# Moving the first chunk's key reads to ScalarE, and a stack clear and a split to GpSimd, in the prologue of an attention-and-experts kernel

## The chip, the cores and the metric

The kernel runs on one core of one Trainium2 chip. The metric is the device time of one launch in microseconds (us), as the median of several runs. Before the change three runs gave 858.39, 859.47 and 859.04 us, a median of 859.04 us.

## The reference, cut to what matters

One block of a gated cross-attention layer and a routed expert layer, on 32 sequences of 128 tokens and width 128, all in float32:

```python
x = x + tanh(g_xattn) * xattn(layernorm(x), ctx, ...)
x = x + tanh(g_ffn) * ffn(layernorm(x), ...)

def xattn(x, xa, ...):                  # 16 heads of 8
    q, k, v    = heads(x @ Wqkv + bqkv)
    _, ka, va  = heads(xa @ Wqkv_aux + bqkv_aux)
    p, pa = softmax(q k' / sqrt(8)), softmax(q ka' / sqrt(8))
    out = (p v) * (1 - sigmoid(g)) + (pa va) * sigmoid(g)
    return out @ Wo + bo
def ffn(x, ...):                        # 64 experts of width 64, top 8 of 4 groups, and a shared one
    return sum_e w[:, e] * (silu(x @ Wg[e]) * (x @ Wu[e])) @ Wd[e] + shared(x)
```

Only the attention, and of it only its first sequences, is touched by the change.

## The kernel before

The 32 sequences are taken in 16 pairs; `n` is a pair, `b = 2n + c` a sequence. The attention runs over all pairs first, the experts follow. Each of the five engine queues (`on_sp`, `on_pool`, `on_act`, `on_dve`, `on_pe`) is a list written out by hand. Each engine takes its list strictly in order and waits on semaphores, so an instruction that waits holds back everything behind it on its engine, DMA issues included.

**What a pair needs.** The layer norm of x (`norm_stats`, `root` with its power on GpSimd, `norm`), a transpose on TensorE (`transposes`) evacuated by ScalarE (`evac_t`), and the projections `project_qk`, `project_ka`, `project_v`. ScalarE copies q and k out of PSUM (`copy_q`, `copy_k`) and, for the first two pairs, also ka (`copy_first_ka`). The scores are computed from bf16 parts: `split` takes a float32 tile apart into three bf16 parts with four instructions in a row (L1167, L1170, L1172, L1174 on VectorE; L609, L612, L614, L616 on GpSimd). A pair has three splits: one of q, and one of k and ka for each of its two sequences. Each counts `lo_ok` up by one.

**The stacks.** The parts go to a DRAM scratch and come back in the order in which the score matmuls want them, in `stack_q[s]` and `stack_k[s]`, three buffers of each. Pair 0 is the "first chunk": its parts are stored by `store_first_q`, `store_first_k(c)` and read back by `load_first(c)`, four `load_products` calls of two DMAs each (L414 and L417) for one sequence: q of head half 1, q of half 0, k of half 1, k of half 0. Pair 1 follows in the same queue with `store_q(1, 1)`, `store_k(1, 1)`, `load_stack_q(1)`, `load_stack_k(1)`. All of these are issued by SyncE, one behind the other. Before their first load the stacks are filled once with zeros or with `kones`: `stack_k[0]` and `stack_k[1]` by VectorE (`clear_stack`, L936), the q stacks and the third k stack by ScalarE.

**The prologue** is what lies ahead of the first `body`. TensorE computes the scores of sequences 0 and 1 (`first_scores`, L1308, four rounds each), VectorE takes the maxima of each round (`first_maxima`, L997) and from them the shift of the exponent (`minus_max`, L1005), and one round's scores must wait until the maxima of the round before the last are taken. The first `body` begins on TensorE with the shifted scores of sequence 0 (`shifted`, L1323), laced with the scores of sequence 2 (`scores`, L1294). For these it waits on three things:

```python
            if c == 0:
                wait(pe, stk[S_HEAD[u] // HH][s], 64 * ...)      # stack_there(2, 0): half 1 of pair 1's stacks
            if j == 0:
                wait(pe, mx_ok, UNITS * b + u - 1)               # scores(2, 0, 0): all maxima of sequences 0 and 1
            if u == 0 and j == 0:
                wait(pe, shift, 16 * (b + 1))                    # shifted(0, 0, 0): the shift rows of sequence 0
```

`clear_v(1)` on GpSimd sets the second buffer `V` to zero (L640) and its columns of ones; `gate_consts` on VectorE makes the gates that GpSimd then multiplies into `wo` (L656, L660). These are needed by `bias_of_v`, in the second quarter of the first body.

Of the kernel before, what the change touches and what calls it, by code (L numbers as in the profile page):

```python
# [16 lines left out]
F32 = mybir.dt.float32  # L17
# [7 lines left out]
P = 128  # L25
# [146 lines left out]
def attention(nc, sem, m, m_cw, psum, v):  # L172
# [131 lines left out]
    q_first, k_first = sem("first_q_parts_stored"), [sem(f"first_k_parts_stored{c}") for c in range(CH)]  # L304
# [66 lines left out]

    def weight_loads(sp):

        sp.dma_start(wqkv[:], v["Wqkv"].rearrange("d (o n) -> d o n", o=3)).then_inc(w_qkv_in, 16)
        sp.dma_start(wqkva[:], v["Wqkv_aux"].rearrange("d (o n) -> d o n", o=3)).then_inc(w_qkv_in, 16)

    def bias_loads(sp):

        turned = lambda a: a.rearrange("(h d a) -> d h a", d=DH, a=1)
        for i, b in enumerate((turned(v["bqkv"][0:P]), turned(v["bqkv"][P:2 * P]), turned(v["bqkv_aux"][P:2 * P]))):  # L380
            sp.dma_start(bcol[:, i:i + 1], b, allow_slow_non_contiguous=True).then_inc(c_in, 16)

# [9 lines left out]
    def on_sp(sp):  # L392
# [17 lines left out]
        def load_products(to, rows, keys, half, width, done):  # L410
            own = rows[:, half * width:(half + 1) * width]
            mixed = own if keys else own[DH:]
            step = DH if keys else 0
            sp.dma_start(to[0:4 * DH], bass.AP(mixed.tensor, mixed.offset,  # L414
                                               [[2 * width, 2 * DH], [step * 2 * width, 2], [1, width]])).then_inc(done, 16)
            plain = own[DH:3 * DH] if keys else own[0:2 * DH]
            sp.dma_start(to[4 * DH:6 * DH], plain).then_inc(done, 16)  # L417

        def load_stack_q(n):

            s = n % NST
            wait(sp, st_mm, UNITS * CH * (n - NST + 1))
            wait(sp, q_st[n % 2], 16 * ((n + 1) // 2))
            for half in (1, 0):
                load_products(stack_q[s][PARTS_AT[half]:PARTS_AT[half] + ROWS_S].rearrange("p h c t -> p (h c t)"),
                              q_v[n], False, half, HH * TC, stk[half][s])

        def load_stack_k(n):

            s = n % NST  # L430
            wait(sp, st_mm, UNITS * CH * (n - NST + 1))
            wait(sp, k_st[n % 2], 16 * ((n + 1) // 2))
            for half in (1, 0):
                load_products(stack_k[s][PARTS_AT[half]:PARTS_AT[half] + ROWS_S].rearrange("p h c a t -> p (h c a t)"),
                              k_v[n], True, half, 2 * HH * TC, stk[half][s])

        def store_first_q():

            wait(sp, lo_ok, 1)
            for c in range(CH):  # L440
                src = parts_q[0][:, :, c * P:(c + 1) * P]
                sp.dma_start(q0_d[c].rearrange("s p t -> p s t"), src).then_inc(q_first, 16)
# [6 lines left out]

        def load_first(c):  # L450

            wait(sp, q_first, 32)
            for half in (1, 0):
                load_products(q_of(0)[PARTS_AT[half]:PARTS_AT[half] + ROWS_S, :, c].rearrange("p h t -> p (h t)"),
                              q0_v[c], False, half, HH * P, stk0[half][c])
            wait(sp, k_first[c], 16)
            for half in (1, 0):
                load_products(k_of(0)[PARTS_AT[half]:PARTS_AT[half] + ROWS_S, :, c].rearrange("p h a t -> p (h a t)"),
                              k0_v[c], True, half, 2 * HH * P, stk0[half][c])
# [106 lines left out]
    def on_pool(pool):  # L566
# [28 lines left out]
        def split(n, half, c):  # L595
# [7 lines left out]
            if n == 2 and half == 0:  # L603
                wait(pool, q_first, 32)
# [43 lines left out]
        root(1)  # L648
        pool.wait_ge(xn_ok, 2)
        root(2)  # L650
        pool.wait_ge(lo_ok, SPLITS * 2)
# [11 lines left out]
        clear_v(1)  # L663
        pool.memset(f_mhalf[:], -0.5).then_inc(fc_ok, 1)
        pool.wait_ge(fc_ok, 1)
        pool.memset(f_gtop[:], HIGH).then_inc(fc_ok, 1)
# [51 lines left out]
    def on_act(act):  # L718
# [130 lines left out]
        copy_k(1)  # L849
        copy_first_ka(1)  # L850
        act.wait_ge(v_zero, 3)
# [67 lines left out]
    def on_dve(dve):  # L919
# [12 lines left out]
        def clear_stack(i):  # L932

            for a in range(2):
                one_col = kones[:, 2 * a:2 * a + 2].bitcast(F32).unsqueeze(1).to_broadcast([P, HH * CH, P // 2])
                ins = nc.vector.tensor_copy(stack_k[i][:].rearrange("p h c a t -> p (h c) a t")[:, :, a, :].bitcast(F32), one_col)  # L936
            ins.then_inc(stack_zero, 1)
# [253 lines left out]
        split(1, 1, 1, 1)  # L1191
        for r in range(ROUNDS):
            first_maxima(0, r)
        minus_max(0, 0, 3)
# [53 lines left out]
    def on_pe(pe):  # L1248
# [162 lines left out]
        wait(pe, t_ev, 2)  # L1411
        transposes(2, 0)
        first_scores(0, 0)
# [696 lines left out]
```

## Time and profile before

| what | value |
|---|---|
| median of 3 runs | 859.04 us |
| the profiled execution's own time | 859.58 us |
| its span in the profile | 857.8 us |
| TensorE busy | 826.2 us, 96% of the span |
| VectorE / ScalarE / GpSimd busy | 683.6 / 566.8 / 637.3 us |
| share of TensorE in the chain that ended last | 87% |
| start of the first `body` on TensorE | 36.43 us |

The span is what the hardware profiler saw between the first and the last instruction; the execution's own time has 1.8 us more around it. A row of the timeline gives start, duration (both us), engine, line, operation, what it writes and reads, a count when like instructions were merged, and in brackets how long the engine stood idle before it and what released it. "SPq" and "ACTq" are DMA issues of SyncE and ScalarE.

### The profile page before, as it was taken

The page shows a single profiled execution, that of the slowest core. Times are in us where ns is not written, and L with a number is a line of the kernel's source. Part 1 is how long each engine was busy: PE and PEld are TensorE (multiplying, and loading weights), DVE is VectorE, ACT ScalarE, POOL GpSimd, SP SyncE. Part 2 cuts the span into 40 slices and gives each one's busy share as a digit, 9 for nine tenths or more (in the row PEclk, how much of TensorE's full clock was granted, in tenths as well). Part 3 has the DMA queues.
Part 4 walks back from the last instruction along what each step waited for, and adds up shares of the span by engine and source line. Part 5 has one row for each costly group of instructions (what it writes and reads, how often), then busy time and mean ns, then how long its engine had stood idle before and what let it go on. Part 6 is the DMA issues. An engine that isn't in the chain of part 4 may idle for free.

```text
span 857.8 us, 20206 instructions
## 1 busy us (share of the span) xinstructions
PE 826.2 (96%) x6733; PEld 646.0 (75%) x6733; DVE 683.6 (80%) x1648; ACT 566.8 (66%) x964; POOL 637.3 (74%) x602
## 2 busy tenths in 40 slices
PE   4899999999999999999999999999999999999997
PEld 3477777777766678888888888878888888888885
DVE  6789999999897769769678877867966977876665
ACT  4388888888878665575576576557557557655554
POOL 2668888888854378877787786777777788778785
PEclk8599999999999999999999999999999999999999
DMA  4677786776652167447456554654654755546562
GB/s 119 173 169 173 178 183 155 187 169 170 160 126 51 53 152 169 120 111 184 117 142 147 131 142 125 154 135 109 163 139 111 171 130 134 149 116 150 137 138 58
DMA packets 108036, 120.04 MB, mean 140 GB/s; under 512 B 28560, under 2 KB 70352, under 8 KB 106496
## 3 DMA queue, kind: packets, MB, share of 16 engines
q1 hardware_dynamic: 105056, 118.23, 57.5%
q10 hardware_dynamic: 2880, 0.59, 0.4%
q8 instruction: 49, 0.80, 0.4%
q14 instruction: 51, 0.42, 0.2%
HBM read 103.55 MB, written 14.71 MB: 138 GB/s over the span
## 4 chain that ended last, share of the span: by engine, by line
PE 87%; DVE 5%; DMA 3%; issue 2%; SPq 1%; ACT 1%; POOL 0%; DVEq 0%; POOLq 0%
PE bank L1999 20%; PE bank L2000 20%; PE bank L2001 20%; PE bank L1336 7%; PE bank L1323 5%; PE bank L1294 3%; PE bank L1276 2%; PE bank L1344 2%; PE bank L1260 1%; PE bank L1357 1%; DVE mx L989 1%; PE bank L1270 1%; DMA cwb<-wts_scratch 1%; DMA stack_q<-nmaxT 1%; PE bank L1976 1%
## 5 line engine op out<-in xcount | busy, mean ns | idle before, releaser
L1676 POOL TENSOR_TENSOR hid<-act,cwb 128x512 f32<-128x512 f32 x264 | 424.0, 1615 | 126.4 <-DVE act L1903 69.1
L1729 ACT ACTIVATE silu<-bank 128x512 f32<-128x512 f32 x256 | 152.9, 597 | 190.7 <-PE bank L2001 189.9
L1903 DVE TENSOR_TENSOR act<-silu,bank 128x512 f32<-128x512 f32 (+1 forms) x264 | 180.5, 684 | 119.5 <-ACT silu L1729 78.7
L1999 PE MATMUL bank<-xhi,weights_hi 128*128 128x512 f32 x520 | 206.6, 397 | 0.0
L1911 DVE TENSOR_TENSOR hlo<-hid,hhi 128x512 fp32r<-128x512 f32 x256 | 197.5, 772 | 8.5 <-ACT hhi L1735 8.3
L2001 PE MATMUL bank<-xlo,weights_hi 128*128 128x512 f32 x520 | 204.2, 393 | 0.0
L2000 PE MATMUL bank<-xhi,weights_lo 128*128 128x512 f32 x520 | 203.9, 392 | 0.0
L1735 ACT ACTIVATE hhi<-hid 128x512 fp32r<-128x512 f32 (+1 forms) x264 | 164.8, 625 | 15.7 <-POOL hid L1676 13.1
L989 DVE TENSOR_REDUCE mx<-bank 128x4 f32<-128x512 f32 x240 | 156.0, 683 | 16.6 <-PE bank L1294 14.8
L786 ACT ACTIVATE prob<-bank 128x1024 f32<-128x1024 f32 x128 | 131.2, 1025 | 48.6 <-PE bank L1323 46.5
L2001 PEld LDWEIGHTS bank<-xlo,weights_hi 128*128 128x128 f32 x520 | 97.6, 188 | 22.0
L1999 PEld LDWEIGHTS bank<-xhi,weights_hi 128*128 128x128 f32 x520 | 97.6, 188 | 21.3 <-ACT silu L1729 0.4
L2000 PEld LDWEIGHTS bank<-xhi,weights_lo 128*128 128x128 f32 x520 | 97.8, 188 | 20.3
L1999 PE MATMUL bank<-hhi,weights_hi 128*128 128x512 f32 x256 | 101.1, 395 | 4.5 <-DVE hlo L1911 4.4
L2000 PE MATMUL bank<-hhi,weights_lo 128*128 128x512 f32 x256 | 100.3, 392 | 0.0
L2001 PE MATMUL bank<-hlo,weights_hi 128*128 128x512 f32 x256 | 99.9, 390 | 0.0
L1323 PE MATMUL bank<-stack_q,stack_k 52*128 52x128 bf16 (+1 forms) x1024 | 80.0, 218 | 7.4 <-DMA stack_k<-k_scratch 2.7
L1323 PEld LDWEIGHTS bank<-stack_q,stack_k 52*128 52x128 bf16 (+1 forms) x1024 | 58.0, 94 | 33.6 <-issue 13.9
L1336 PE MATMUL bank<-prob,V 128*32 128x128 f32 x2048 | 82.5, 279 | 0.1
L1294 PE MATMUL bank<-stack_k,stack_q 52*128 52x256 bf16 (+1 forms) x480 | 74.8, 274 | 0.4 <-DVE mx L989 0.2
L1336 PEld LDWEIGHTS bank<-prob,V 128*32 128x32 f32 x2048 | 48.1, 109 | 17.9 <-issue 11.1
L1999 PEld LDWEIGHTS bank<-hhi,weights_hi 128*128 128x128 f32 x256 | 48.0, 187 | 17.8 <-DVE hlo L1911 6.6
(238 smaller groups left out, 1022.1 us busy)
## 6 DMA issues: line engine op xcount, KB each, us to landing
cwb<-wts_scratch SPq DMA_DIRECT2D x174, 384.0 KB, 5.4
stack_k<-k_scratch SPq DMA_DIRECT2D x30, 256.0 KB, 4.3
k_scratch<-parts_k SPq DMA_DIRECT2D x15, 384.0 KB, 3.4
stack_q<-q_scratch SPq DMA_DIRECT2D x30, 128.0 KB, 2.9
stack_k<-k_scratch SPq DMA_DIRECT2D x30, 128.0 KB, 5.2
q_scratch<-parts_q SPq DMA_DIRECT2D x15, 192.0 KB, 2.7
xin<-in_x_dram SPq DMA_DIRECT2D x16, 128.0 KB, 3.0
cin<-in_ctx_dram SPq DMA_DIRECT2D x16, 128.0 KB, 3.1
```

The costliest lines, as they stand in the source:

```text
L786: act.activation(prob[pair % RP][:].rearrange("p u k -> p (u k)"), wide[:], ACT.Exp, scale=scale).then_inc(p_ok, 1)
L989: nc.vector.tensor_reduce(mx[par][:, 2 * f:2 * f + 2, h:h + 2].rearrange("p a h -> p h a"), s_bank[u % 2][:].rearrange("p (h a k) -> p h a ...
L1323: ins = nc.tensor.matmul(st_bank[u % 2][:, j * P:(j + 1) * P], k_of(n)[at, h % HH, c, a, :], q_of(n)[at, h % HH, c, :], start=True, stop=True)
L1336: ins = nc.tensor.matmul(o_bank[par][VW * j:VW * (j + 1), (u // 2) * P:(u // 2 + 1) * P], V[i][:, a, par, h0 + j, :], prob[(ROUNDS * b + u ...
L1676: pool.tensor_tensor(h_buf[k][:], a_buf[k][:], cwb[slot][:, q % GP, :], ALU.mult).then_inc(h_ok, 1)
L1729: act.activation(s_buf[k % RS][:], g_bank[k % 2][:], ACT.Silu).then_inc(s_ok, 1)
L1735: act.activation(hhi[k % RH][at], h_buf[k % RS][at], ACT.Copy).then_inc(hh_ok, 1)
L1903: nc.vector.tensor_tensor(a_buf[k % RS][at], s_buf[k % RS][at], u_bank[k % 3][at], ALU.mult).then_inc(a_ok, 1)
L1911: nc.vector.tensor_tensor(hlo[k % RH][:], h_buf[k % RS][:], hhi[k % RH][:].bitcast(F32), ALU.subtract).then_inc(hl_ok, 1)
L1999: nc.tensor.matmul(bank, w[0], mh, start=first, stop=False)
L2000: nc.tensor.matmul(bank, w[1], mh, start=False, stop=False)
L2001: return nc.tensor.matmul(bank, w[0], ml, start=False, stop=last)
```

## The change

- `load_products` becomes a helper with the issuing engine as argument; `load_first(c)` is replaced by `load_first_q(eng, c, half)` and `load_first_k(eng, c, half)`. `store_first_q` counts one semaphore for each sequence, so that a q read waits for its own sequence's store only.
- ScalarE issues three of the four key reads of the first chunk: (0, half 1) between `copy_k(1)` and `copy_first_ka(1)`; (0, half 0) and (1, half 1) after it. SyncE keeps the four q reads and the key read (1, half 0), and `store_first_k(1)` moves up to stand behind the first q read.
- GpSimd clears `stack_k[1]` with two copies and then does `clear_v(1)` and the `f_` memsets, all right after `root(1)`; VectorE no longer does `clear_stack(1)`.
- GpSimd takes the last split of pair 1 (`split(1, 1, 1)`); VectorE keeps the other five of pairs 0 and 1. `split(1, 1, 0, 0)` moves ahead of `norm_stats(2)`, `split(1, 1, 1, 0)` ahead of `norm(2)`, and `gate_consts` behind the first round of maxima.
- TensorE does `first_scores(0, 0)` ahead of `transposes(2, 0)`.

```diff
+    def load_products(eng, to, rows, keys, half, width, done):
+        own = rows[:, half * width:(half + 1) * width]
+        mixed = own if keys else own[DH:]
+        step = DH if keys else 0
+        eng.dma_start(to[0:4 * DH], bass.AP(mixed.tensor, mixed.offset,
+                                           [[2 * width, 2 * DH], [step * 2 * width, 2], [1, width]])).then_inc(done, 16)
+        plain = own[DH:3 * DH] if keys else own[0:2 * DH]
+        eng.dma_start(to[4 * DH:6 * DH], plain).then_inc(done, 16)
+
+    def load_first_q(eng, c, half):
+        wait(eng, q_first[c], 16)
+        eng.wait_ge(stack_clear, 1)
+        load_products(eng, q_of(0)[PARTS_AT[half]:PARTS_AT[half] + ROWS_S, :, c].rearrange("p h t -> p (h t)"),
+                      q0_v[c], False, half, HH * P, stk0[half][c])
+
+    def load_first_k(eng, c, half):
+        wait(eng, k_first[c], 16)
+        eng.wait_ge(stack_zero, 1)
+        load_products(eng, k_of(0)[PARTS_AT[half]:PARTS_AT[half] + ROWS_S, :, c].rearrange("p h a t -> p (h a t)"),
+                      k0_v[c], True, half, 2 * HH * P, stk0[half][c])
+    def one_rows(i, a):
+        to = stack_k[i][:].rearrange("p h c a t -> p (h c) a t")[:, :, a, :].bitcast(F32)
+        return to, kones[:, 2 * a:2 * a + 2].bitcast(F32).unsqueeze(1).to_broadcast([P, HH * CH, P // 2])
...
@@ on_sp
         store_first_q()
         store_first_k(0)
+        load_first_q(sp, 0, 1)
+        store_first_k(1)
+        load_first_q(sp, 0, 0)
+        load_first_q(sp, 1, 1)
+        load_first_q(sp, 1, 0)
+        load_first_k(sp, 1, 0)
         sp.wait_ge(stack_zero, 2)
         sp.wait_ge(stack_clear, 2)
-        load_first(0)
-        store_first_k(1)
-        load_first(1)
         store_q(1, 1)
         store_k(1, 1)
@@ on_pool
         root(1)
+        pool.wait_ge(kones_rows, 1)
+        pool.wait_ge(stack_zero, 1)
+        for a in range(2):
+            ins = pool.tensor_copy(*one_rows(1, a))
+        ins.then_inc(stack_zero, 1)
+        clear_v(1)
+        pool.memset(f_mhalf[:], -0.5).then_inc(fc_ok, 1)
+        pool.wait_ge(fc_ok, 1)
+        pool.memset(f_gtop[:], HIGH).then_inc(fc_ok, 1)
         pool.wait_ge(xn_ok, 2)
         root(2)
-        pool.wait_ge(lo_ok, SPLITS * 2)
+        pool.wait_ge(lo_ok, SPLITS * 2 - 1)
+        split(1, 1, 1)
...
@@ on_act
         copy_k(1)
+        load_first_k(act, 0, 1)
         copy_first_ka(1)
+        load_first_k(act, 0, 0)
+        load_first_k(act, 1, 1)
         act.wait_ge(v_zero, 3)
         copy_v(0, 0)
         evac_t(2, 0)
@@ on_dve
-        clear_stack(0)
+        clear_stack()
         norm_stats(1)
         norm(1)
-        clear_stack(1)
         split(0, 0, 0, 0)
         split(0, 0, 1, 0)
         split(0, 0, 1, 1)
+        split(1, 1, 0, 0)
         norm_stats(2)
-        split(1, 1, 0, 0)
+        split(1, 1, 1, 0)
         norm(2)
-        gate_consts()
-        split(1, 1, 1, 0)
-        split(1, 1, 1, 1)
         for r in range(ROUNDS):
             first_maxima(0, r)
+            if r == 0:
+                gate_consts()
@@ on_pe
+        first_scores(0, 0)
         transposes(2, 0)
-        first_scores(0, 0)
         first_scores(0, 1)
```

## Rows read from the trace of the kernel before

**Rows 1.** The profile's page: chain that ended last, shares by engine.

```profile
PE 87%; DVE 5%; DMA 3%; issue 2%; SPq 1%; ACT 1%; POOL 0%; DVEq 0%; POOLq 0%
```

**Rows 2.** Chain that ended last, in order of time: start, us, what.

```profile
21.71 0.56 SPq L414
...
31.96 4.42 DMA stack_k<-k_scratch
36.43 0.28 PE bank L1323
```

**Rows 3.** Timeline, maxima of sequences 0 and 1 on VectorE.

```profile
26.38 2.36 DVE L997 TENSOR_REDUCE mx<-bank 128x8 f32<-128x1024 f32 x2 [0.61 <-PE bank L1308]
...
32.94 2.36 DVE L997 TENSOR_REDUCE mx<-bank 128x8 f32<-128x1024 f32 x2
```

**Rows 4.** Timeline, TensorE between the projections and the third round of scores.

```profile
18.80 1.22 PE L1276 MATMUL bank<-wqkv,xcT 128*128 128x128 f32 x4 [0.56 <-ACT full_k L766]
...
20.67 0.63 PE L1253 MATMUL bank<-ident,xn 128*128 128x128 f32 x2
...
22.27 1.89 PE L1308 MATMUL bank<-stack_k,stack_q 52*128 52x256 bf16 x8 [0.54 <-DMA stack_k<-first_k_scratch]
...
24.09 1.22 PE L1260 MATMUL bank<-xcT,wqk 128*128 128x256 f32 x2
...
25.24 1.88 PE L1308 MATMUL bank<-stack_k,stack_q 48*128 48x256 bf16 x8
```

**Rows 5.** Timeline, ScalarE's copies out of PSUM.

```profile
12.89 0.47 ACT L766 ACTIVATE full_k<-bank,bcol 128x256 f32<-128x256 f32 x1 [0.36 <-PE bank L1270]
...
16.43 0.47 ACT L761 ACTIVATE full_k<-bank,bcol 128x256 f32<-128x256 f32 x1 [1.36 <-DVE parts_k L1174]
...
18.28 0.47 ACT L766 ACTIVATE full_k<-bank,bcol 128x256 f32<-128x256 f32 x1 [1.38 <-PE bank L1270]
```

**Rows 6.** DMA issues one by one: KB, us from issue to landing.

```profile
first_k_scratch<-parts_k SPq DMA_DIRECT2D x1, 192.0 KB, 2.0
...
stack_k<-first_k_scratch SPq DMA_DIRECT2D x1, 64.0 KB, 3.2
```

**Rows 7.** Timeline, DMA issues of SyncE and ScalarE.

```profile
14.97 0.36 SPq L448 DMA_DIRECT2D first_k_scratch<-parts_k  x1
...
30.05 1.44 ACTq L780 DMA_DIRECT2D stack_q<-nmaxT  x1
37.97 0.63 ACTq L780 DMA_DIRECT2D stack_q<-nmaxT  x1
```

**Rows 8.** Timeline, VectorE's first splits, those of pair 0.

```profile
11.85 0.29 DVE L1167 CAST parts_q<-full_q 128x256 bf16<-128x256 f32 x1
...
15.97 0.43 DVE L1174 TENSOR_TENSOR parts_k<-rest,parts_k 128x256 bf16<-128x256 f32 x1
```

**Rows 9.** Timeline, GpSimd: what its kinds of work cost.

```profile
1.55 0.29 POOL L572 CAST ident_bf<-ident 128x128 bf16<-128x128 f32 x1
...
9.39 0.70 POOL L582 TENSOR_TENSOR rstd<-var,mhalf 128x2 f32<-128x2 f32 x1 [3.26 <-DVE var L974]
...
17.42 0.70 POOL L582 TENSOR_TENSOR rstd<-var,mhalf 128x2 f32<-128x2 f32 x1 [7.33 <-DVE var L974]
...
24.33 1.80 POOL L640 MEMSET V<- 128x2048 f32 x1
...
33.20 0.61 POOL L609 TENSOR_TENSOR parts_k<-full_k,ones 128x256 bf16<-128x256 f32 x1
```

**Rows 10.** Timeline, a small VectorE instruction without and beside GpSimd work.

```profile
290.08 0.17 DVE L1797 TENSOR_SCALAR f_negm<-f_mv 128x4 f32<-128x4 f32 x1
...
361.60 1.80 POOL L1676 TENSOR_TENSOR hid<-act,cwb 128x512 f32<-128x512 f32 x1 [0.24 <-DVE act L1903]
362.57 0.86 DVE L1797 TENSOR_SCALAR f_negm<-f_mv 128x4 f32<-128x4 f32 x1
```

**Rows 11.** Windows of 1 us: length, busy time of PE, PEld, DVE, ACT, POOL, granted clock, DMA.

```profile
39.00:40.00 1.00, 1.00 (x14) 0.78 (x13) 0.00 (x0) 0.00 (x0) 0.00 (x0) 0.59 0.07 16
```

More of the change, by code:

```diff
@@ L303, in attention @@
     k_st = [sem(f"k_parts_stored{i}") for i in range(2)]
-    q_first, k_first = sem("first_q_parts_stored"), [sem(f"first_k_parts_stored{c}") for c in range(CH)]
+    q_first, k_first = ([sem(f"first_{n}_parts_stored{c}") for c in range(CH)] for n in "qk")
     stk0 = [[sem(f"first_stack_half{a}_loaded{c}") for c in range(CH)] for a in range(2)]
@@ L408, in store_k @@
             sp.dma_start(k_d[n].rearrange("s p c a t -> p s (c a t)"), parts_k[i][:]).then_inc(k_st[i], 16)
[L410 to L417, printed above, removed]
         def load_stack_q(n):
@@ L424, in load_stack_q @@
             for half in (1, 0):
-                load_products(stack_q[s][PARTS_AT[half]:PARTS_AT[half] + ROWS_S].rearrange("p h c t -> p (h c t)"),
+                load_products(sp, stack_q[s][PARTS_AT[half]:PARTS_AT[half] + ROWS_S].rearrange("p h c t -> p (h c t)"),
                               q_v[n], False, half, HH * TC, stk[half][s])
@@ L433, in load_stack_k @@
             for half in (1, 0):
-                load_products(stack_k[s][PARTS_AT[half]:PARTS_AT[half] + ROWS_S].rearrange("p h c a t -> p (h c a t)"),
+                load_products(sp, stack_k[s][PARTS_AT[half]:PARTS_AT[half] + ROWS_S].rearrange("p h c a t -> p (h c a t)"),
                               k_v[n], True, half, 2 * HH * TC, stk[half][s])
@@ L441, in store_first_q @@
                 src = parts_q[0][:, :, c * P:(c + 1) * P]
-                sp.dma_start(q0_d[c].rearrange("s p t -> p s t"), src).then_inc(q_first, 16)
+                sp.dma_start(q0_d[c].rearrange("s p t -> p s t"), src).then_inc(q_first[c], 16)
         def store_first_k(c):
@@ L448, in store_first_k @@
             sp.dma_start(k0_d[c].rearrange("s p a t -> p s (a t)"), src).then_inc(k_first[c], 16)
[L450 to L459, printed above, removed]
         def expert_weights(g, j):
@@ L603, in split @@
             if n == 2 and half == 0:
-                wait(pool, q_first, 32)
+                for done in q_first:
+                    wait(pool, done, 16)
             elif n == 2:
@@ L662, in on_pool @@
         pool.wait_ge(wo_ok, 4)
[L663 to L666, printed above, removed]
         pool.wait_ge(fc_ok, 2)
@@ L930, in shift_rows_of_k, with clear_stack @@
             dve.wait_ge(kones_rows, 1)
-        def clear_stack(i):
+        def clear_stack():
             for a in range(2):
-                one_col = kones[:, 2 * a:2 * a + 2].bitcast(F32).unsqueeze(1).to_broadcast([P, HH * CH, P // 2])
-                ins = nc.vector.tensor_copy(stack_k[i][:].rearrange("p h c a t -> p (h c) a t")[:, :, a, :].bitcast(F32), one_col)
+                ins = nc.vector.tensor_copy(*one_rows(0, a))
             ins.then_inc(stack_zero, 1)
```

## The prediction, made before the changed kernel was run

> **What bounds the kernel now.** I read the page first. The chain that ended last is TensorE for 87% of the span [rows 1], so after the prologue the kernel is a belt of matmuls: what starts it earlier ends it earlier, one for one. Everything that the change touches lies ahead of the first body or at its edge, so I then read the chain in order of time up to there. It runs through SyncE's issues of the first chunk's reads, which begin with the DMA issue at 21.71 us, through the store and reload of pair 1, and ends in a read of `stack_k` that is issued at 31.96 and lands 4.42 us later; TensorE begins the body at 36.43 [rows 2]. The second question is what would come next if that read came early. The body also waits for the last maxima of sequences 0 and 1. They are done at 32.94 + 2.36 = 35.30, and from the third round of sequence 0 at 26.38 on VectorE works without a gap worth naming, 8.92 us for this stretch [rows 3]. So the queue of SyncE gives at most 36.43 - 35.35 = 1.08 us, and more only if the maxima come earlier too.
>
> The maxima hang on TensorE [rows 4]: the values of pair 0 are projected from 18.80, as soon as ScalarE's second ka copy is out [rows 5], the third transposes follow at 20.67, the first scores at 22.27 after 0.54 us idle for a read of `stack_k`, a projection at 24.09, and the third round of scores at 25.24. Two rounds of scores take 24.09 - 22.27 = 1.82, one 0.91; four transposes about 0.86 (two of them start 0.43 after the other two); the projection 1.15.
>
> **The change part by part.** I count time from how late VectorE has finished the three splits of pair 0. Before, that is at 15.97 + 0.43 = 16.40 [rows 8]. Call the lateness against 16.40 after the change D. ScalarE's `copy_k(1)` waits for it (16.43), the ka projection waits for that, and the second ka copy at 18.28 for the projection [rows 5], so D moves this whole chain.
>
> (a) Key reads on ScalarE, with D = 0. The store of the parts of sequence 0 is issued at 14.97 [rows 7] and lands 2.0 us later [rows 6], at 16.97. ScalarE's copy ends at 16.90, so it waits 0.07 us. An issue on ScalarE takes 0.63 [rows 7], so two end at 18.2, just ahead of 18.28, when the ka copy can go: nothing is lost behind them. The second is issued at 17.6 and lands 3.2 us later [rows 6], at 20.8. The four issues after the ka copy end at about 21.3; behind them stand `copy_v(0, 0)`, whose matmuls end near 20.9, and `evac_t(2, 0)`, which is not due before 22.7. They are covered. If an issue takes 1.44 us, as one of ScalarE's does [rows 7], the read lands at 21.6 and the ka copy is 0.8 late: a cost of 0.8 us at most; I take nothing, since only one of the two rows is that long.
>
> (b) First scores ahead of the third transposes. TensorE is through with the values at 20.67 [rows 4]; the scores start at 20.8. Then 0.91 + 0.86 + 0.91, and the projection starts at 23.48 instead of 24.09: 0.61 us earlier. The transposes need the norm of pair 2: VectorE is at that point with one more split and the two norms, by 20.85, against a need at 21.7; covered by 0.85 us. The third round of scores and the last maxima move with the projection, to 35.30 - 0.61 = 34.69. `gate_consts` (0.55 us) lies between the first and the second round of maxima, while TensorE transposes; without that cover it would cost its 0.55.
>
> (c) SyncE's queue. It is free of the first chunk's reads near 21.9 instead of 26.6, the store of pair 1's keys waits for GpSimd's split (four instructions of about 0.65 with gaps, 2.8 us, instead of 1.5 on VectorE, ended near 23.2), and even with the longest reload shown, 4.42 us [rows 2], the half that the body wants lands near 31.4. It is off the path by 3 us, and every us of D moves both. So the maxima decide, and the body starts at 34.75: a gain of 1.68 - D. The later GpSimd work (`wo`, the splits of pair 2) is either earlier or hangs on the same projection.
>
> (d) The clear and the memsets on GpSimd, which is where D comes from. VectorE loses the clear that stood ahead of its q split, which may start with ScalarE's q copy near 11.4 instead of at 11.85 [rows 8]; but the k split behind it waits for the ka copy that ends at 12.89 + 0.47 = 13.36 [rows 5], as it did before, so the saving ends there: D is never below 0. GpSimd is through with `root(1)` at 10.09 [rows 9] and then copies twice 128x1024. The trace has no such copy. From below: a memset of 2048 elements takes 1.80 us [rows 9], 0.9 for 1024. From above: a two-input instruction of 256 takes 0.61 [rows 9], 2.4 us for 1024. A one-input cast of 128 takes 0.29 [rows 9], near the memset's rate and a small fixed part, so I take 1.05 us each: 10.15 to 12.25. Then comes the memset of `V`, 1.80.
>
> Does that hold VectorE up? A tensor_scalar of 4 elements takes 0.17 us with GpSimd idle, and 0.86 when a GpSimd instruction is in flight; it then ends with that one, at 363.43 against 363.40 [rows 10]. It has one input in SBUF, like the casts of a split. Against it stands the root at 17.42, beside which a split of pair 1 ran at full speed; but it has two elements a partition [rows 9]. So I take the two copies as blocking: the q split starts at 12.25, not 11.4. At 1.53 us a split (11.85 to 16.40 for three, [rows 8]) the q split ends at 13.8, 0.4 late. The trace shows no memset beside a cast. From below it blocks nothing and D = 0.4; from above the second cast of the q split, due at 13.0, waits until the memset ends at 14.3, the split ends at 15.0, and D = 1.6. I take the upper end: the instruction that was held had only one input, so it isn't only a clash of reads.
>
> The Trainium skill (SBUF — State Buffer, "Who interferes with whom") says that VectorE in its two-port modes and GpSimd share a pair of ports, and that "the other fully blocks", while a VectorE instruction with two SBUF inputs doesn't clash with a GpSimd one that only writes. By that page the memset holds the casts and not the subtractions, which gives the same D = 1.6; the trace agrees for GpSimd instructions that read, and no run here shows it yet for a memset.
>
> The sum: 36.43 - 34.75 - 1.6 = 0.1 us gained at the start of the body. The profiled execution of before took 859.58 with a span of 857.8; the median lies 0.54 lower, and I take the gain from the median: 859.04 - 0.1 = 858.9 us.
>
> **The clock.** In the body's first 3.4 us TensorE runs at 1.2 GHz; between 39 and 40 us the granted clock goes from 0.5 to 1 [rows 11], that is to 2.4 GHz. If the body starts earlier and the clock rises at the same moment, up to half of the gain is lost again. It costs nothing here, because the start hardly moves, and up to 0.8 us in the rival with the largest gain.
>
> **The rivals.**
> - *Only the copies block, not the memset* (or nothing does): D = 0.4 (or 0), a gain of 1.3 (or 1.7) at the start of the body: 857.8 (857.4). For it: the trace has no held instruction beside a memset. Against it: the row above. If the clock's rise stays where it is, 858.4.
> - *The copies are slow* (slower than before). At the two-input rate, 2.4 us each, VectorE gets one cast in between them at 12.6, is held by the second until 15, then by the memset until 17.2, and D is about 4.6: 2.9 us slower, 862.0. It loses over 0.2% from a copy of about 2 us on. For it: the broadcast source has an odd shape. Against it: the cast's 0.29.
> - *ScalarE's issues are slow or the key read lands late*: 0.8 us on top of D = 1.6 gives 859.7 (858.9 + 0.8); still no change that can be told.
> - *The change doesn't move the start at all*, because TensorE was waiting for the shift rows, whose landing the trace doesn't show: 859.0.
>
> **How the numbers follow.** 0.2% is 1.7 us, about what a measurement of this kernel can tell from no change. Chances: forecast (D about 1.6) 0.42; only copies or nothing blocks 0.33, of which a third could pass 1.7 us with the clock's help; slow issues or unmoved start 0.13; slow copies or another stall of over 1.7 us 0.12. So faster 0.13, same 0.75, slower 0.12. The range reaches from 857.3, the case without any hold, to 860.2, a copy of some 1.4 us together with slow issues.
>
> **What would show it.** In the changed profile: GpSimd's two copies between 10.1 and 12.3 and its memset until about 14; a cast of VectorE (first of the q split) that is long and ends with the second copy, and the next cast long and ending with the memset; pair 0's splits done near 18.0; first scores on TensorE near 22.4, the third round of scores near 26.2; maxima done near 36.3; the body near 36.4, waiting on VectorE's maxima and no longer on a DMA; reads of `stack_k` for pair 1 landed by 33. The step most likely to be wrong is the hold by the memset: casts at 0.29 beside it would make the body start at 35.1. I would also be wrong if ScalarE's two issues delay the ka copy past the start of the values, or if the splits of pair 2 on GpSimd come late enough to stall the third body.

## The result, and the profile after

The changed kernel takes 860.86 us (median of 15 runs, 859.01 to 863.54), the kernel before 859.2 us in the same comparison. The ratio is 1.0019, with a 95% interval of 1.0011 to 1.0027: about 1.6 us slower, where 858.9 and no change had been forecast. Medians below are over all executions of a kernel, ratios leave out the single ones of 1.15 to 4.40 ms. The profiled execution of the changed kernel took 859.84 us with a span of 858.0. Its chain by engine, from the page, beside [rows 1]:

```profile
PE 88%; DVE 5%; issue 2%; DMA 2%; ACT 1%; SPq 0%; POOL 0%; ACTq 0%; DVEq 0%; POOLq 0%
```

The timeline of the changed kernel from the second norm to the first matmul of the body:

```profile
10.08 2.02 POOL L662 COPY stack_k<-kones 128x1024 f32<-128x1024 f32 x2
10.16 2.01 DVE L998 TENSOR_SCALAR xn<-xin,mv,rstd 128x128 f32<-128x128 f32 x2 [0.89 <-POOL rstd L591]
12.04 1.88 POOL L650 MEMSET V<- 128x2048 f32 x1
12.10 1.97 DVE L1185 CAST parts_q<-full_q 128x256 bf16<-128x256 f32 x1
...
14.24 0.47 ACT L782 ACTIVATE full_k<-bank,bcol 128x256 f32<-128x256 f32 x1 [0.26 <-PE bank L1287]
14.56 0.29 DVE L1190 CAST parts_q<-rest 128x256 bf16<-128x256 f32 x1
...
17.79 0.42 DVE L1192 TENSOR_TENSOR parts_k<-rest,parts_k 128x256 bf16<-128x256 f32 x1
18.25 0.47 ACT L777 ACTIVATE full_k<-bank,bcol 128x256 f32<-128x256 f32 x1 [0.90 <-DVE parts_k L1192]
...
20.14 0.47 ACT L782 ACTIVATE full_k<-bank,bcol 128x256 f32<-128x256 f32 x1 [1.42 <-PE bank L1287]
...
26.80 1.88 PE L1325 MATMUL bank<-stack_k,stack_q 48*128 48x256 bf16 x8
...
31.61 1.21 ACTq L796 DMA_DIRECT2D stack_q<-nmaxT  x1
...
34.50 2.36 DVE L1015 TENSOR_REDUCE mx<-bank 128x8 f32<-128x1024 f32 x2
...
37.09 0.26 PE L1340 MATMUL bank<-stack_q,stack_k 64*128 64x128 bf16 x1 [1.85 <-DMA stack_q<-nmaxT]
```

Read it from the top. GpSimd's two copies take 2.02 us together, and the norm of pair 1 on VectorE, 0.60 before, takes 2.01 and ends with them. The memset follows at once, and the first cast of the q split, 0.29 in [rows 8], takes 1.97 and ends with it. The second cast takes 0.29 again. The splits of pair 0 end at 17.79 + 0.42 = 18.21, not 16.40 as in [rows 8]. The third round of scores starts at 26.80 against 25.24 [rows 4], the last maxima end at 36.86 against 35.30 [rows 3], and the body starts at 37.09 against 36.43 [rows 2]. What releases it is neither a maximum nor a read of `stack_k` but the 16 KB of shift rows.

The chain in order of time of the same execution, at the places where the change sits (start, us, what):

```profile
16.79 2.03 DMA first_k_scratch<-parts_k
18.84 0.62 ACTq L376
19.50 0.60 ACTq L379
20.14 0.48 ACT full_k L782
20.67 2.08 PE bank L1293 x8
22.75 0.96 PE bank L1325 x4
23.71 0.62 PE bank L1270 x2
24.33 0.43 PE bank L1272 x2
24.76 0.96 PE bank L1325 x4
25.72 1.15 PE bank L1277 x2
...
40.92 0.11 PE bank L1340
41.02 0.06 PE bank L1311
```

The last two lines read TensorE's clock: a matmul of the first body moves the chain by 0.11 us until 41.0 and by 0.05 to 0.06 behind it, 1.2 GHz and then 2.4 GHz. The column of the granted clock says 1.00 throughout here and in several other profiles, so the level is read from the length of like matmuls. In the profile of the kernel before, whose column does show it, the granted clock rises at 39.8, in the window of [rows 11].

**One profile is not the median.** This profiled execution is 1.0 us below its kernel's median and starts the body 0.66 us late, which doesn't account for 1.6. So I read two more of the changed kernel and one more of the kernel before (runs below), and one place behind the clock's rise: the first matmul that waits for `prob` after 43 us. The row of each kernel, first of the kernel before:

```profile
45.31 0.21 PE L1323 MATMUL bank<-stack_q,stack_k 64*128 64x128 bf16 x1 [0.66 <-ACT prob L786]
```

and of the changed kernel:

```profile
46.19 0.21 PE L1340 MATMUL bank<-stack_q,stack_k 64*128 64x128 bf16 x1 [0.66 <-ACT prob L802]
```

| | body starts | clock rises | this matmul |
|---|---|---|---|
| before, two profiles | 36.43, 35.69 | 39.8, 41.0 | 45.31, 45.06 |
| changed, three profiles | 37.09, 37.23, 37.63 | 40.9, 43.4, 43.9 | 46.19, 46.97, 47.45 |

The means of the last column are 45.19 and 46.87, a difference of 1.68 us, the size of the timed one. Up to 80 us the lead or lag of a profile moves by some 0.2 us; by the end of the span it has drifted by up to 1.0 us, one way or the other, with no pattern between the kernels. The difference of the marks is made in the prologue and at the clock's rise.

**The zero of the prediction was early.** The ka projection of pair 0, in the first profile of the kernel before and then in its second (e11):

```profile
11.87 0.99 PE L1270 MATMUL bank<-xcT,wqk 128*128 128x256 f32 x2
```

```profile
11.85 1.19 PE L1270 MATMUL bank<-xcT,wqk 128*128 128x256 f32 x2
```

In the first profile TensorE's clock rose during this projection (the four matmuls behind it take 1.13 us, in e11 2.08), and the ka copy that waits for it starts at 12.89, in e11 at 13.08. Counted from the start of pair 1's norm, the splits of pair 0 end after 6.27 us in the first profile (16.40 - 10.13), after 6.47 in e11 (16.58 - 10.11), and after 6.47 or 6.48 in e1, e3, e5 and e6 below, where nothing holds the norm. In the three profiles of the changed kernel they end after 8.05 or 8.06. So the prediction's D, the lateness of the splits, is 8.05 - 6.47 = 1.58 us.

### The profile page after: what moved, and what is told of

It reads as the page before. It is cut to its first block, busy times and chain, and to the rows that moved or that the text cites. A ratio compares the mean times of both kernels' runs of the same rounds, so it can differ in the third digit from the quotient of the medians.

```text
span 858.0 us, 20217 instructions
## 1 busy us (share of the span) xinstructions
PE 827.3 (96%) x6733; PEld 646.6 (75%) x6733; DVE 684.0 (80%) x1642; ACT 565.9 (66%) x964; POOL 643.0 (75%) x608
## 4 chain that ended last, share of the span: by engine, by line
PE 88%; DVE 5%; issue 2%; DMA 2%; ACT 1%; SPq 0%; POOL 0%; ACTq 0%; DVEq 0%; POOLq 0%
PE bank L2016 20%; PE bank L2018 20%; PE bank L2017 20%; PE bank L1353 7%; PE bank L1340 5%; PE bank L1311 3%; PE bank L1293 2%; PE bank L1361 2%; PE bank L1277 1%; PE bank L1374 1%; PE bank L1287 1%; DVE mx L1007 1%; DMA cwb<-wts_scratch 1%; PE bank L1375 1%; PE bank L1367 1%
## 5 line engine op out<-in xcount | busy, mean ns | idle before, releaser
L2018 PEld LDWEIGHTS bank<-xlo,weights_hi 128*128 128x128 f32 x520 | 97.6, 188 | 21.9
```

The source lines that it names most:

```text
L2018: return nc.tensor.matmul(bank, w[0], ml, start=False, stop=last)
```

## The experiments

All of them compute the whole reference. A diff shows the lines that carry the edit, "..." stands for lines left out. "Mark" is the start of the matmul above in the kernel's own profile, to be held against 45.19 for the kernel before and 46.87 for the changed one.

**e1: GpSimd's early work undone.** VectorE clears `stack_k[1]` behind `norm(1)` again, the memsets go back to their old place; all else stays changed.

```diff
@@ on_pool, after root(1)
...
-        for a in range(2):
-            ins = pool.tensor_copy(*one_rows(1, a))
...
-        clear_v(1)
...
@@ on_pool, after wo_ok
+        clear_v(1)
...
@@ on_dve, after norm(1)
+        for a in range(2):
+            ins = nc.vector.tensor_copy(*one_rows(1, a))
...
```

> The changed kernel with GpSimd's early work undone: the clear of stack_k[1] goes back to VectorE behind the norm of pair 1, and the memset of V[1] and the two small ones go back behind wo; key reads, splits and TensorE's order stay as changed. Theory 1 (GpSimd's copies and memset hold VectorE's norm and first cast, some 1.8 us): the norm of pair 1 takes 0.6 us again instead of 2.0, pair 0's splits end near 16.4 instead of 18.2, the maxima end near 35.0 instead of 36.9, the body starts 1.5 to 2 us earlier than in the changed kernel (37.1), near 35.3; about 1.9 us faster than the changed kernel, ratio to the kernel before 0.998 to 0.999. Rival (ScalarE's DMA issues or TensorE's order cost the time): the splits end earlier, but the body does not start before 36.4, and the ratio stays at 1.001 or more.

858.34 us, ratio to before 0.9993 (0.9983 to 1.0003), body at 35.27, mark 44.73. Timeline of e1:

```profile
10.09 0.60 DVE L993 TENSOR_SCALAR xn<-xin,mv,rstd 128x128 f32<-128x128 f32 x2 [0.88 <-POOL rstd L591]
...
35.27 0.26 PE L1338 MATMUL bank<-stack_q,stack_k 64*128 64x128 bf16 x1 [1.67 <-DVE mx L1010]
```

The norm is short again, and the maxima, which end at 35.21, release the body. The rest of the change is worth some 0.8 us at the body's start against the 36.06 of the kernel before (mean of 36.43 and 35.69), and what was put on GpSimd costs 2.05 us there (37.32, the mean of three, against 35.27) and about 2.2 in the timed ratios (1.0019 against 0.9993). Of the 2.05, 1.65 lie ahead of the end of the maxima (36.86, the mean of three, against 35.21); the other 0.40 are the wait for the shift rows.

**e2: only the memsets back.** The copies stay on GpSimd behind `root(1)`.

```diff
@@ on_pool, after root(1)
-        clear_v(1)
...
@@ on_pool, after wo_ok
+        clear_v(1)
...
```

> The changed kernel with only the memset of V[1] and the two small ones put back behind wo; the two copies on GpSimd stay where they are. Theory 1: the norm of pair 1 is still held by the copies and takes 2.0 us, but the first cast of the q split takes 0.3 instead of 2.0. Since the transposes and the ka copy behind the norm stay about 1.4 us late, pair 0's splits end near 17.8 instead of 18.2 and the body starts only 0.4 to 0.5 us earlier than in the changed kernel, near 36.6. Rival, as the prediction had it (the memset is most of the loss, the copies cost 0.4): splits end near 16.8 and the body starts 1.3 us earlier, near 35.8.

860.91 us, ratio 1.0018 (1.0009 to 1.0027). Timeline of e2:

```profile
10.00 2.02 POOL L662 COPY stack_k<-kones 128x1024 f32<-128x1024 f32 x2
10.08 2.01 DVE L998 TENSOR_SCALAR xn<-xin,mv,rstd 128x128 f32<-128x128 f32 x2 [0.88 <-POOL rstd L591]
...
17.22 0.43 DVE L1192 TENSOR_TENSOR parts_k<-rest,parts_k 128x256 bf16<-128x256 f32 x1
```

The copies alone hold the norm for the full 2 us. The splits end at 17.65, 7.57 us after the norm's start, so the copies make them 7.57 - 6.47 = 1.10 us late, and the memset adds 8.05 - 7.57 = 0.48. The ratio is the changed kernel's own (1.0019); a gain of 0.48 us, 0.0006 of the time, lies within the two intervals and can't be seen in it. Its body start (34.67) and mark (44.64) can't be held against the others: in this one execution TensorE's clock was high from 23.9 to 30.7 us, and rounds of scores that take 1.03 elsewhere took 0.61.

**e3: the same work on GpSimd, later.** Both copies behind `split(1, 1, 1)`, the memsets behind pair 2's splits.

```diff
@@ on_pool
         root(1)
+        root(2)
+        split(1, 1, 1)
         for a in range(2):
             ins = pool.tensor_copy(*one_rows(1, a))
-        clear_v(1)
-        root(2)
-        split(1, 1, 1)
...
         splits(2)
+        clear_v(1)
@@ on_sp
-        sp.wait_ge(stack_zero, 2)
         sp.wait_ge(stack_clear, 2)
...
+        sp.wait_ge(stack_zero, 2)
         load_stack_k(1)
```

> The changed kernel with GpSimd's copies moved behind its split of pair 1, the memsets behind the splits of pair 2, and SyncE's wait for the copies moved to just before the reload of pair 1's keys; VectorE does no second clear. Theory 1: nothing runs on GpSimd beside VectorE's norm and casts of pair 0, the splits end at 16.4, the first scores start near 20.9, the maxima end near 34.8. The body starts near 35.0 if the shift rows have landed by then, 2 us earlier than in the changed kernel; ratio to the kernel before about 0.998. If the shift rows' DMA (5.35 us from issue to landing in the changed kernel, beside the reload of pair 1's keys) sets the end, the body starts at 29.7 + 5.3 = 35.1 or later, and TensorE's wait is put down to it.

858.92 us, ratio 0.9995 (0.9984 to 1.0006), body at 35.69, mark 44.89. The body is released by the shift rows here too, issued at 30.07 and 5.48 us under way; the maxima end at 35.33. Timeline of e3:

```profile
10.15 0.61 DVE L998 TENSOR_SCALAR xn<-xin,mv,rstd 128x128 f32<-128x128 f32 x2 [0.88 <-POOL rstd L591]
...
23.47 2.02 POOL L666 COPY stack_k<-kones 128x1024 f32<-128x1024 f32 x2
24.29 1.23 DVE L1015 TENSOR_REDUCE mx<-bank 128x8 f32<-128x1024 f32 x1 [0.32 <-PE bank L1325]
```

The same copies now cost VectorE nothing: the maxima beside them, which read PSUM, take 1.23 as in the changed kernel, where no copy lies beside them. The three small instructions of `gate_consts` that run from 23.42 on, on 1 or 2 elements a partition, take 0.15 to 0.17, as in the kernel before. It is where the work lies that costs.

**e4: the kernel before with GpSimd's early work alone.**

```diff
@@ on_pool, after root(1)
+        for a in range(2):
+            one_col = kones[:, 2 * a:2 * a + 2].bitcast(F32)
...
+        clear_v(1)
...
@@ on_dve
         norm(1)
-        clear_stack(1)
```

> The kernel before with one part of the change alone: GpSimd clears stack_k[1] and V[1] right behind root(1), VectorE does not. Theory 1: norm of pair 1 2.0 us, first cast 2.0 us, pair 0's splits end near 18.2 instead of 16.4, and since SyncE's queue follows them, the body starts 1.5 to 1.8 us later than before, near 38.1; ratio to the kernel before about 1.002. Rival (the holds are covered by the clear that VectorE no longer does, and by SyncE's queue): body near 36.4 to 36.8, ratio 1.000.

862.41 us, ratio 1.0031 (1.0017 to 1.0045), body at 38.35, mark 47.42. Timeline, then chain of e4:

```profile
10.21 2.01 DVE L986 TENSOR_SCALAR xn<-xin,mv,rstd 128x128 f32<-128x128 f32 x2 [0.89 <-POOL rstd L582]
```

```profile
34.17 4.13 DMA stack_k<-k_scratch
38.35 0.29 PE bank L1328
```

With the old queue of SyncE the lateness goes through to the reload of pair 1, and grows beyond the 1.57 us by which the splits are late: the first q read is issued at 17.84 against 15.84 in e11, the last key read that the body needs at 34.17 against 31.53, and the body starts 2.7 us later than in e11 and 1.9 later than in the first profile of the kernel before.

**e5: the key reads on ScalarE and the new order on SyncE alone.** SyncE's list is that of the change; GpSimd, VectorE and TensorE work as before.

```diff
@@ on_act
         copy_k(1)
+        load_first_k(act, 0, 1)
         copy_first_ka(1)
+        load_first_k(act, 0, 0)
+        load_first_k(act, 1, 1)
```

> The kernel before with one part of the change alone: ScalarE issues three of the four key reads of the first chunk, and SyncE's list is as changed. Clears, splits, norms and TensorE's order are those before. Theory 2 (the freed SyncE queue is the whole gain of the change, and it ends at the maxima): pair 1's keys land near 31.5, the maxima end near 35.1 (0.2 earlier, since the first scores no longer wait for their keys but the transposes stand ahead of them), the body starts near 35.3, waiting for VectorE or for the shift rows; 1.1 us earlier than before, of which the slower start of the clock takes up to half: ratio 0.999. Rival (the freed queue gives nothing, since the shift rows' DMA holds the body as long as the key read did): body at 36.0 or later, ratio 1.000.

859.08 us, ratio 1.0001 (0.999 to 1.0013), body at 35.11, released by VectorE's maxima, mark 44.24. TensorE keeps its old order here and has the keys in time. From the values to the third round of scores, in e5 and then in e1, which has the new order:

```profile
19.13 1.22 PE L1290 MATMUL bank<-wqkv,xcT 128*128 128x128 f32 x4 [0.62 <-ACT full_k L776]
...
24.96 1.88 PE L1322 MATMUL bank<-stack_k,stack_q 48*128 48x256 bf16 x8
```

```profile
19.02 1.22 PE L1291 MATMUL bank<-wqkv,xcT 128*128 128x128 f32 x4 [0.61 <-ACT full_k L777]
...
25.15 1.88 PE L1323 MATMUL bank<-stack_k,stack_q 48*128 48x256 bf16 x8
```

That is 5.83 us in the old order and 6.13 in the new one, with the clock at its low level and no wait in either. The chains show where the 0.30 goes: the transposes take 0.86 and the two rounds behind them 1.82 in e5, and with the transposes between the rounds 0.96, 1.05 and 0.96 in e1. The earlier key reads had already removed the wait that the new order was to fill.

**e6: TensorE's order alone.**

```diff
-        transposes(2, 0)
         first_scores(0, 0)
+        transposes(2, 0)
```

> The kernel before with one part of the change alone: first_scores(0, 0) ahead of transposes(2, 0). The keys still land near 22.2, so the transposes wait for them too: the third round of scores starts near 26.4 instead of 25.2 (0.96 + 1.05 + 0.96 + 1.15 after 22.27, as the changed kernel shows), the maxima end near 36.4 instead of 35.3, and the body starts near 36.5 to 36.8, since the shift rows' DMA follows as well: 0.1 to 0.4 us later, ratio 1.000 to 1.0005. Rival, as the prediction had it (transposes cost 0.86 and fill a wait): third round near 26.1, body unmoved at 36.4.

859.4 us, ratio 0.9999 (0.9989 to 1.0009), body at 36.09, mark 46.02. Timeline of e6:

```profile
22.25 1.01 PE L1308 MATMUL bank<-stack_k,stack_q 52*128 52x256 bf16 x4 [1.09 <-DMA stack_k<-first_k_scratch]
```

Without the earlier key reads the transposes no longer fill the wait, which grows from 0.54 [rows 4] to 1.09, and the third round, at 26.35, comes 1.1 us later than in [rows 4] and 1.5 later than in e11 (24.82). The body's first matmul goes ahead at 36.09, its first scores wait for the maxima until 36.47. So the new order pays neither alone nor, by e5 and e1, together with the earlier key reads.

**e7: e3, with the first key read back on SyncE, and half 0 of pair 1's keys read behind the shift rows.**

```diff
@@ load_stack_k, against e3
+                if n == 1 and half == 0:
+                    sp.wait_ge(shift, 16)
@@ on_sp
         store_first_k(1)
+        load_first_k(sp, 0, 1)
@@ on_act
-        load_first_k(act, 0, 1)
```

> The late-clears kernel with the first key read (sequence 0, half 1) issued by SyncE behind the second key store instead of by ScalarE ahead of the ka copy, and with the last two reads of pair 1's keys waiting for the shift rows to land. Theory 3 (ScalarE's two issues delay the ka copy by 0.2 us, and the shift rows are slow because they share the DMA engines with those reads): the ka copy starts right behind its matmul, the first scores near 20.9, the shift rows land 3 us or less after their issue instead of 5.5, the maxima set the body's start near 35.1, 0.6 us earlier than in the late-clears kernel (35.7). Rival: the shift rows land 5 us after issue whatever else is in flight, and the body starts at 35.5 or later. Ratio to the kernel before 0.999.

859.01 us, ratio 0.9989 (0.9978 to 1.0001), mark 43.83. Its ratio is the lowest of all; by its interval it may still be no change, and it can't be told from e1 and e3. The clock was high from 22.9 to 29.8 in its profile, and the body, at 34.23, was held by the read of `stack_k` issued at 29.52.

**e8: the kernel before with the memsets alone behind `root(1)`** (one profile).

```diff
         root(1)
+        clear_v(1)
...
```

> The kernel before with the memset of V[1] (128x2048) and the small ones right behind root(1); both clears of stack_k stay on VectorE. It tells whether a GpSimd instruction that only writes holds a VectorE instruction with one input. If it does (theory 1): the norm of pair 1 or the copies of the clear behind it end with the memset near 11.95, the q split starts near 13.2 instead of 11.85, pair 0's splits end 1 to 1.4 us late. If only instructions that read hold VectorE, the norm takes 0.6, the clear 1.29, and the q split starts at 11.85.

860.96 us, body at 37.56, mark 46.87. Timeline of e8:

```profile
10.13 1.80 POOL L640 MEMSET V<- 128x2048 f32 x1
10.22 1.86 DVE L980 TENSOR_SCALAR xn<-xin,mv,rstd 128x128 f32<-128x128 f32 x2 [0.88 <-POOL rstd L582]
```

A GpSimd instruction that reads nothing stretches the norm from 0.60 to 1.86. The splits of pair 0 end at 17.75, 7.53 us after the norm's start: the memset alone makes them 1.06 us late.

**e9, e10, e11: the changed kernel twice more and the kernel before once more**, unedited.

> The changed kernel once more, for a second profile. Open is why it is 1.6 us slower by the median when its first profile shows only 0.66 us at the body's start. If the first profile was a lucky execution (theory 4: what scatters is when the granted clock rises after the body's start, 3.4 to 6.3 us in the profiles so far, and when the shift rows land), this one shows the body at 37 or later, the clock's rise anywhere from 40.5 to 43.5, and a matmul in the middle of the attention 0.8 to 2.5 us later than in the kernel before. If the loss lies behind the prologue (rival), the body starts at 37.1 with an early rise and TensorE loses a further us at some later place that the kernel before does not lose.

> The same as the one before, a third profile of the changed kernel: body at 37.0 to 37.5, the clock's rise at another moment than in the other two, the mid-attention matmul later or earlier by half of the difference between the rises.

> The kernel before once more, for a second profile. Theory 4: pair 0's splits end at 16.4 and the body starts between 36.2 and 36.8 as in the first, since SyncE's queue sets it and not TensorE's clock; the clock's rise scatters as in the others, between 39.8 and 43. Rival: the body's start itself scatters by a us or more from the landing of pair 1's keys.

861.09, 862.52 and 859.72 us. The chain of e9 and then of e11 at the body's start:

```profile
31.64 5.45 DMA stack_q<-nmaxT
...
37.23 0.26 PE bank L1340
```

```profile
31.53 4.11 DMA stack_k<-k_scratch
35.69 0.28 PE bank L1323
```

The expectation for e11 missed: its body starts at 35.69, below 36.2, though its splits end later than in the first profile. Its keys of the first chunk are there without a wait, the third round starts at 24.82 (5.83 us after the values, as in e5), and the reload of pair 1 is issued 0.43 earlier and lands 0.31 faster. The shift rows hold the changed kernel's body in all three profiles (in e10 they are issued at 31.56 and take 5.93, and the body starts at 37.63), and the first one had their shortest landing (5.35) and much the earliest rise of the clock. The timeline of e9 shows the late rise: the same 16 matmuls take 1.08 us at 42.35 and 0.65 two us later.

```profile
42.35 1.08 PE L1353 MATMUL bank<-prob,V 128*32 128x128 f32 x16
...
44.50 0.65 PE L1353 MATMUL bank<-prob,V 128*32 128x128 f32 x16
```

**e12: the changed kernel, with half 0 of pair 1's keys read behind the shift rows.**

```diff
@@ load_stack_k
+                if n == 1 and half == 0:
+                    sp.wait_ge(shift, 16)
```

> The changed kernel with one wait more: SyncE issues the reads of half 0 of pair 1's keys only when the shift rows of sequence 0 have landed. Nothing else differs, so the norm of pair 1 (2.01 us), the splits of pair 0 (ended near 18.2) and the maxima (ended near 36.9) stay as in the changed kernel. Theory A: the shift rows take 5.35 to 5.93 us from issue to landing because two larger reads of keys are put in the queues around them; then their landing takes about 3 us here, at about 34.6, the body starts as soon as the last maxima are taken, at 36.9 to 37.0, and the time is 0.2 to 0.6 us below the changed kernel's. Theory B: they take over 5 us by themselves; then they land at 37.0 as before, the reads of half 0 are issued near 37, land past 41, and TensorE waits for them in the first body, so that the kernel is over 1 us slower than the changed one. Both: slower than before the change, by 0.1 to 0.2% in A.

861.55 us, ratio 1.0008 (0.9994 to 1.0022), mark 45.77. Timeline of e12:

```profile
31.59 1.22 ACTq L798 DMA_DIRECT2D stack_q<-nmaxT  x1
...
34.44 0.55 SPq L376 DMA_DIRECT2D stack_k<-k_scratch  x1
...
36.90 0.39 PE L1313 MATMUL bank<-stack_k,stack_q 52*128 52x256 bf16 x1 [0.83 <-DVE mx L1017]
```

SyncE, waiting for the shift rows, goes on at 34.44: they have landed 2.85 us after their issue, not 5.35 to 5.93, and the scores of the body start at 36.90 with the end of the maxima. The expectation's theory A held. The norm is 2.02 here, as in the changed kernel. (This profiled execution, 862.22, lost 1.7 us more at 310 us, where the granted clock fell to 0.5 for a while.)

| kernel | mark - 45.19 | timed, (ratio - 1) x 859.5 us, interval |
|---|---|---|
| changed | +1.68 (three) | +1.6 (+0.9 to +2.3) |
| e1 | -0.46 | -0.6 (-1.5 to +0.3) |
| e2 (high clock from 23.9 to 30.7) | -0.55 | +1.5 (+0.8 to +2.3) |
| e3 | -0.30 | -0.4 (-1.4 to +0.5) |
| e4 | +2.23 | +2.7 (+1.5 to +3.9) |
| e5 | -0.95 | +0.1 (-0.9 to +1.1) |
| e6 | +0.83 | -0.1 (-0.9 to +0.8) |
| e7 (high clock from 22.9 to 29.8) | -1.36 | -0.9 (-1.9 to +0.1) |
| e12 | +0.58 | +0.7 (-0.5 to +1.9) |

One mark of one execution scatters by up to 1.3 us (46.19 to 47.45 of one kernel). The marks of e1, e3, e4 and e12 go with their times; those of e5 and e6 lie one us to either side of a time that didn't change, which that scatter and the intervals allow but don't show.

## Why the prediction was wrong

**The forecast's range missed**: 860.86 lies 0.66 above its upper end of 860.2. The sum of the prediction was a gain of 1.68 us at the body's start less D. D came out as forecast, 1.58 against 1.6. The step that failed is the other term, "So the maxima decide, and the body starts at 34.75: a gain of 1.68 - D": without GpSimd's early work (e1) the gain is 0.8 us, and with that work a wait for the shift rows comes on top of D, which the sum had at nothing.

By the prediction the body was to start at 34.75 + 1.6 = 36.35. It starts at 37.32 (mean of three). From one to the other, in order of the steps:

- *The zero*: 0.21. The 16.40 of [rows 8], from which D was counted, comes from an execution in which TensorE's clock rose during the ka projection. Without a hold the splits end 6.47 us behind the norm's start, in the changed kernel's profile at 16.63; they end 1.58 later, at 18.21 instead of 16.40 + 1.6 = 18.00.
- *(b), the order on TensorE*: 0.30. From the values at 20.67 to the third round it is 6.13 us. The prediction took 0.61 off the 6.44 of its one profile, which comes to 5.83. Those 5.83 us are what the old order takes once the keys are in time (e5, and e11 even with the old reads). The new order itself costs 0.30: a round measured 0.96 and the transposes 1.05 where they alternate, and 0.91 and 0.86, as the prediction had read them, where they don't. The lacing of `gate_consts` cost nothing.
- *The shift rows*: 0.42. They were named as a rival, as part of a case of 0.13 and at the price of no change, and they came on top: with the reads of pair 1's keys issued from 30.06, they and the shift rows (31.61) are under way together. In e12, where half of those reads stay back, the body's scores start at 36.90, with the end of the maxima.
- *Small steps* between the third round and the end of the maxima: 0.04.

0.21 + 0.30 + 0.42 + 0.04 = 0.97. To this come 0.37 from the kernel before, whose one profile had a late body (36.43 against 36.06 in the mean of two), and 0.42 from what lies between the body's start and the mark (9.13 us before, 9.55 changed, in the means), where the clock's rise falls. Together with the forecast's own gain of 0.08: 0.97 + 0.37 + 0.42 - 0.08 = 1.68, the difference of the marks. The terms of the shift rows, of the kernel before and of the mark rest on two or three profiles only.

**D was right by luck.** Its two parts were wrong in opposite ways. "So I take the two copies as blocking: the q split starts at 12.25, not 11.4" left the norm of pair 1 at its old 0.60 beside the copies, and put their cost at 0.4. They hold the norm, and with it pair 1's transposes and the ka copy, which starts at 14.24 and not at 12.89 [rows 5]; that is 1.10 without any memset (e2). The memset does block, as forecast, but the first cast and for 0.48 more, not 1.2. In the same way "no change that can be told", below the 0.2% that the prediction drew as its line, still holds for a ratio of 1.0019, but only just, and not for the reason given. The copies' price, 1.05 each, measured 1.01.

**What was right.** (a): ScalarE's second ka copy starts 1.89 us after the k copy, against 1.85 before: its two issues cost 0.04, and the bound of 0.8 and the rival of slow issues fall. The landing of the key store, at 18.82, now sits in the chain with them, so they have no slack left. (c): SyncE's queue is off the path. It is free at 24.3, where 21.9 and D make 23.5. With D, the half of pair 1's keys that the body wants was to land near 33; its last read, issued at 30.66, takes 4.2 us and lands near 34.9, 2 us ahead of the end of the maxima instead of 3. (d), that GpSimd holds VectorE's casts and its tensor_scalar, a memset too, is shown by e8 and by the changed kernel.

**The shared ports.** The rule that I cited, the Trainium skill (SBUF — State Buffer, "Who interferes with whom"), held as far as it was tried: the instructions that were stretched are a tensor_scalar and a cast. No subtraction lay beside a long memset; the only one beside a memset, at 14.10 and beside short ones of 32 elements, kept its 0.42. The same section names `tensor_scalar` beside copy and cast among those that can take the shared ports. Whether the norm, with its two scalars for each partition, was one of them no row of the kernel before showed; the page's sentence was there to ask the question, and I asked it of the casts alone. The trace agrees with it: 2.01 us against 0.60.

**The clock.** The forecast said that an earlier start is given back by up to half if the rise stays where it is. A late start isn't given back: the clock rises 3.8, 6.2 and 6.3 us after the body's start in the three profiles of the changed kernel, and 3.4 and 5.3 us after it in those of the kernel before. Why a rise comes early or late isn't settled.

**What stays open.** e5 starts the body 0.95 us earlier (35.11 against 36.06) and times as no change; with an interval of one us to each side, I can't say whether the gain is real and lost in the scatter. The cost of the new order, 0.30 us, is read from profiles and lies below what the timed ratios can show; e1 with the old order was not run. And e12 shows that holding back 384 of the reads' 768 KB brings the shift rows in 2.5 us earlier, but not whether it is their order in the engines' queues or shared bandwidth.

## What to carry to other kernels

GpSimd is a free engine only where VectorE is reading PSUM or standing still: before clearing a buffer there, list every VectorE copy, cast and tensor_scalar in those microseconds, norms with scalar operands too, and follow what hangs on each. Here the same two copies made the splits 1.1 us late beside a norm, and cost nothing 13 us later beside the maxima. A filler pays only while the wait that it fills is there: once the key reads came early, moving the transposes between the rounds cost 0.30 us. When the bound is a start of a long belt, look for the small transfer that is issued last (here 16 KB of shift rows), and take several profiles of both kernels before sizing a difference of one us from them: the zero and two of the waits of this prediction were those of one execution.

## What the runs showed of the hardware

- A memset of 2048 elements a partition on GpSimd, which reads nothing, held a float32 tensor_scalar of VectorE with scalar operands from 0.60 to 1.86 us, and a cast from 0.29 to 1.97. The held instruction ended with the GpSimd one, within 0.15 us.
- GpSimd copied 128x1024 float32 from a broadcast source in 1.01 us.
- A DMA of 16 KB took 5.35, 5.45 and 5.93 us from issue to landing among reads of 128 and 256 KB on another queue, 2.85 us with half of these held back (e12).
- On TensorE, four transposes and then two rounds of four score matmuls (52x256) took 0.86 + 1.82 us at 1.2 GHz (e5), the same with the transposes between the rounds 0.96 + 1.05 + 0.96 (e1).
- The rise of TensorE's clock came 3.4 to 6.3 us after the start of the same body, and moved by 3.0 us between executions of one kernel.
- The column of the granted clock read 1.00 throughout the prologue of executions in which 16 like matmuls took 1.08 us and 0.65 two us later (e9).
